# Linear attention in 64-wide TensorE tiles: one change to a fused patch, attention and expert kernel

## The chip, the cores and the metric

The kernel runs on one core of a Trainium2 chip. The metric is the time of one execution on the device, in microseconds (us); lower is better. Five engines work side by side and meet at semaphores: PE (TensorE: matmuls and transposes, with the load of their stationary operand listed apart as PEld), DVE (VectorE), ACT (ScalarE), POOL (GpSimd) and SP (which issues DMAs).

## The reference, cut to what matters

64 images of 96x96x3 are cut into 36 patches each and projected to 256 features; a class token and 77 text tokens are added, which makes 114 tokens an image. Then come a linear attention of 16 heads of 16 features, and 8 experts of which each token takes one. The part that the change touches is the middle of the attention:

```python
Q = _feature_map(Q)
K = _feature_map(K)
KV = jnp.einsum('bshd,bshe->bhde', K, V)
K_sum = K.sum(axis=1)
Z = 1.0 / (jnp.einsum('bshd,bhd->bsh', Q, K_sum) + 1e-06)
out = jnp.einsum('bshd,bhde,bsh->bshe', Q, KV, Z)
```

Each head needs only its own 16x16 block of keys times values.

## The kernel before

The images go in 32 pairs. Each engine runs `for i in range(PAIRS): step(i)`, a pipeline written out by hand: the PE `step` (L1482) holds, in this order, `rank(i - 4)`, `key_value(i - 1)`, `turn_attention(i - 2)`, `project(i)`, `project_out(i - 2)`, `apply(i - 1)`, `turn_tokens(i + 1)` and `queries(i)`. DVE (L1171) and ACT (L832) have lists of their own. Nothing is scheduled at run time: an engine waits at its next instruction until the semaphore arrives. After the pairs, 64 tiles of sorted tokens go through the experts (L1580, L1616).

- `key_value` (L1366) multiplies keys by values for an image b and a half c of the heads (8 heads, 128 features): the stationary operand is `k_sb` of 114 tokens x 128 features, and 136 columns of `v_sb` move: 128 values, and 8 ones that give the sums of the keys. Four such matmuls make a pair. They are f32, and each is two passes in the trace, with a load of its own for each pass.
- `masked` (L1030, DVE) multiplies the four 128 x 136 results by a mask that keeps the blocks of each head, into `kv_sb`.
- `apply` (L1429) multiplies queries (`qT`, 128 features x 114 tokens, stationary) by `kv_sb`, 136 columns moving, again four f32 matmuls of two passes.
- `denominators` (L805, ACT) and `attention` (L1078, DVE) take the last 8 columns of each result, invert them and scale the 128 others.
- Around them on PE: `rank` (L1359 to L1362, bf16), the transposes of `turn_attention` (L1389) and `turn_tokens` (L1451), and products of the fp32r kind, written as three matmuls (L1326 to L1328). `queries` writes its results to the bank `b_w`, which `residual` (L1054) and `gate_logits` (L1062) on DVE must have read; `key_value` and `rank` write to `b_att`, which `attention` must have read.
- In two steps there is small extra work on PE ahead of `rank`: `early_count` (L1472) and `early_slots` (L1479, L1480), whose results have 8 rows or 1.

Of the kernel before, what the change touches and what calls it, by code (L numbers as in the profile page):

```python
# [24 lines left out]
P = 128  # L25
# [11 lines left out]
HEADS = 16  # L37
DH = D // HEADS
HPC = P // DH
KVW = P + HPC  # L40
EXPERTS = 8
INNER = 128
REGION = TOKENS + P
# [16 lines left out]
Z_EPS = 1e-6  # L60

CONSTS = {
    "c_ident": (P, P), "c_earlier": (TOK, TOK), "c_mask": (P, KVW), "c_weight8": (TOK, EXPERTS),
    "c_region": (P, 2 * EXPERTS), "c_regcol": (EXPERTS, 1), "c_tri": (EXPERTS, ENDS_W), "c_gap": (EXPERTS, ENDS_W),
    "c_before": (EXPERTS, EXPERTS),
}
# [1 line left out]
SLOT_W = EARLY_TILES * EXPERTS + EARLY_TILES  # L68
ROW_SETS = [range(0, 1), range(1, 2), range(2, 3), range(3, 4), range(4, 6), *(range(n, min(n + 3, 32)) for n in range(6, 32, 3))]
KGW = D + EXPERTS  # L70
RANK_AT, EARLY_AT = KC * KVW, 320
DUO = 2
RESULT_RING = 8
DUOS = TILES // DUO
# [38 lines left out]
def build(nc, x, txt, w_tok, pos, wq, bq, wkgv, wo, wo_rows, bias, drop, bias_kv, bo_col, wgu_in, wdown_in, ids, consts, slots, out):  # L113
    scratch = nc.dram_tensor("sorted_rows", (EXPERTS * REGION + P, ROW), F32, kind="Internal").ap()

    with ExitStack() as ctx:
# [85 lines left out]
        with ExitStack() as room:  # L202
            q_exp = sb("q_exp", [P, KC, 2 * TOK], at=room)
            q_relu = sb("q_relu", [P, KC, 2 * TOK], at=room)
            qT = sb("qT", [P, KC, 2 * TOK], at=room)
            k_exp = sb("k_exp", [TOK, 2, D], at=room)
            k_sb = sb("k_sb", [TOK, 2, D], at=room)
            gate_part = sb("gate_part", [TOK, 4, 2, EXPERTS], at=room)
            v_sb = sb("v_sb", [TOK, 2, KC, KVW], at=room)
            kv_sb = sb("kv_sb", [P, 2, KC, KVW], at=room)  # L210
            den = sb("den", [TOK, 2, HEADS], at=room)
            z = sb("z", [TOK, 2, HEADS], at=room)
            attn = sb("attn", [TOK, 2, D], at=room)
            attnT_hi, attnT_lo = parts("attnT", [P, KC, 2 * TOK], room)
            rows = sb("rows", [TOK, 4, 2, ROW], at=room)
            stats2 = sb("stats2", [TOK, 2, 6], at=room)
            mv2 = sb("mv2", [TOK, 4, 2, 2], at=room)
            ve2 = sb("ve2", [TOK, 2], at=room)
            rstd2 = sb("rstd2", [TOK, 4, 2], at=room)
            mean_neg = sb("mean_neg", [TOK, 4, 2], at=room)  # L220
            ratio = sb("ratio", [TOK, 2], at=room)
            logits = sb("logits", [TOK, 2, 2, EXPERTS], at=room)
            top = sb("top", [TOK, 2, 2], at=room)
            top_n = sb("top_n", [TOK, 2, 2], at=room)
            ranked = sb("ranked", [TOK, 2, EXPERTS], at=room)
            first = sb("first", [TOK, 2], at=room)
            chosen = sb("chosen", [TOK, 2, 2, EXPERTS], BF16, room)
            tanh_top = sb("tanh_top", [TOK, 2, 2], at=room)
            route_w = sb("route_w", [TOK, 2], at=room)
            place_e = sb("place_e", [TOK, 2, EXPERTS], at=room)  # L230
            place_f = sb("place_f", [TOK, 4, 2], at=room)
            place = sb("place", [TOK, 4, 2], I32, room)

            xsT = sb("xsT", [P, 6, KC, P], at=room)
            silu_g = sb("silu_g", [P, 4, INNER], at=room)
            act_u = sb("act_u", [P, 4, INNER], at=room)
            actT = sb("actT", [P, 6, P], at=room)
            result = sb("result", [P, RESULT_RING, D], at=room)
# [15 lines left out]
        b_att = ps("b_att", [P, 2, 512])  # L254
        b_w = ps("b_w", [P, 2, 512])
        b_t = ps("b_t", [P, 512])

        b_x, b_gu = (b_v[:, :], b_t[:, :]), (b_kg[:, 0, :], b_kg[:, 1, :])

# [482 lines left out]
        def _(act):  # L742
# [54 lines left out]
            def values(p):  # L797

                act.wait_ge(kvp_done, p + 1)
                if p >= 1:  # L800
                    act.wait_ge(kvm_done, p)
                S.copy(v_sb[:, :, :, 0:P].rearrange("p b k e -> p (b k) e"),
                       b_v[0:TOK, :].rearrange("p (a e) -> p a e", e=P)).then_inc(v_ready, 1)

            def denominators(p):  # L805

                act.wait_ge(apply_done, p + 1)
                if p >= 1:
                    act.wait_ge(z_done, p)
                heads = b_att[0:TOK, :, 0:KC * KVW].rearrange("p b (k w) -> p b k w", k=KC)  # L810
                S.activation(den[:].rearrange("p b (k h) -> p b k h", k=KC), heads[:, :, :, P:KVW], ACT.Identity,
                             bias=z_eps[0:TOK, :]).then_inc(den_done, 1)

            def tokens_high(p):
# [122 lines left out]
        def _(dve):  # L937
# [92 lines left out]
            def masked(p):  # L1030

                dve.wait_ge(kvm_done, p + 1)
                if p >= 1:
                    dve.wait_ge(apply_done, p)
                V.tensor_tensor(kv_sb[:].rearrange("p b k w -> p (b k) w"),
                                b_att[:, :, 0:KC * KVW].rearrange("p b (k w) -> p b k w", k=KC),
                                mask.rearrange("p (a w) -> p a w", a=1).to_broadcast([P, 2 * KC, KVW]),
                                ALU.mult).then_inc(kv_ready, 1)

            def queries(p):  # L1040
# [37 lines left out]
            def attention(p):  # L1078
# [4 lines left out]
                dve.wait_ge(apply_done, p + 1)  # L1083
                if p >= 1:
                    dve.wait_ge(turn_attn_done, p)
                heads = b_att[0:TOK, :, 0:KC * KVW].rearrange("p b (k w) -> p b k w", k=KC)
                for b in range(2):
                    last = V.tensor_tensor(
                        attn[:, b, :].rearrange("p (k h e) -> p k h e", k=KC, h=HPC),
                        heads[:, b, :, 0:P].rearrange("p k (h e) -> p k h e", h=HPC),  # L1090
                        z[:, b, :].rearrange("p (k h a) -> p k h a", k=KC, a=1).to_broadcast([TOK, KC, HPC, DH]),
                        ALU.mult)
                last.then_inc(attn_ready, 1)

# [128 lines left out]
            def room_setup():  # L1223

                for n in (PT - 2, PT - 1):
                    patches_out(Turn(0, n))
                dve.wait_ge(patches_ready, PT)
                V.memset(v_sb[:, :, :, P:], 1.0)
                V.memset(rows[:, :, :, ID + 1:], 0.0).then_inc(room_ready, 1)

            units(dve, unit, [
# [88 lines left out]
        def _(pe):  # L1320
# [45 lines left out]
            def key_value(p):  # L1366
# [6 lines left out]
                    pe.wait_ge(attn_ready, p)  # L1373
                for b in range(2):
                    for c in range(KC):
                        last = T.matmul(b_att[:, b, c * KVW:(c + 1) * KVW], k_sb[:, b, c * P:(c + 1) * P],  # L1376
                                        v_sb[:, b, c, :], start=True, stop=True)
                last.then_inc(kvm_done, 1)

            def turn_attention(p):  # L1380
# [48 lines left out]
            def apply(p):  # L1429
# [4 lines left out]
                    pe.wait_ge(place_ready, p - 2)  # L1434
                for b in range(2):
                    for c in range(KC):
                        last = T.matmul(b_att[0:TOK, b, c * KVW:(c + 1) * KVW], qT[:, c, b * TOK:(b + 1) * TOK],  # L1437
                                        kv_sb[:, b, c, :], start=True, stop=True)
                last.then_inc(apply_done, 1)

            def turn_tokens(p):
# [236 lines left out]
def constants():  # L1678

    f = np.float32  # L1680
    d, h = np.arange(P), np.arange(HPC)
    own = (d[:, None] // DH == h[None, :]).astype(f)
    e = np.arange(EXPERTS)
    region = np.zeros((P, 2 * EXPERTS), f)
    region[TOK, 0:EXPERTS] = e * REGION
    tables = {
        "c_ident": np.eye(P, dtype=f),
        "c_earlier": np.triu(np.ones((TOK, TOK), f), 1),
        "c_mask": np.concatenate([np.repeat(own, DH, axis=1), own], axis=1),
        "c_weight8": np.tile((EXPERTS - e).astype(f), (TOK, 1)),  # L1690
        "c_region": region,
        "c_regcol": (e * REGION).astype(f)[:, None],
# [107 lines left out]
```

## Time and profile before

| | |
|---|---|
| median of 3 runs | 465.07 us (464.49 to 466.78) |
| the profiled execution's own time | 466.39 us |
| its span, first to last instruction | 464.6 us |
| PE busy | 442.6 us (95%) |
| DVE, POOL, ACT busy | 334.3, 291.5, 265.0 us |
| mean granted TensorE clock | 0.985 |

The profile follows one execution. Its span is the time from the first to the last instruction; the execution's own time has 1.8 us around that. Matmuls are pipelined: a matmul is listed from the moment that it is sent to the array to the moment that its last result is out, so neighbours overlap in the list. What a matmul costs the stream is the distance from its start to the start of the next, not its listed length.

### The profile page before, as it was taken

Reading aid. Unit: us, or ns where it says so; the run is one execution under the profiler, and the core shown is the slowest. Engines: PE = TensorE matmul, PEld = TensorE weight load, DVE = VectorE, ACT = ScalarE, POOL = GpSimd, SP = SyncE. Lnnn points to the kernel's source line nnn. Section 1 sums busy time; section 2 is a strip of 40 time slices with the busy share of each in tenths; the row PEclk is TensorE's granted clock in tenths of the full one; section 3 lists DMA queues with packets and bytes.
Section 4 is the critical chain, followed back from the end, with each engine's and each line's share of the span. In section 5 each row is a group of like instructions: output and inputs, shape, how many; then the busy total and the mean of one; then the engine's idle time right before and its main releaser. Section 6 shows DMA issues by size and latency. Waiting matters only on the chain.

```text
span 464.6 us, 11297 instructions
## 1 busy us (share of the span) xinstructions
PE 442.6 (95%) x3490; PEld 423.6 (91%) x3490; DVE 334.3 (72%) x1115; ACT 265.0 (57%) x640; POOL 291.5 (63%) x662
## 2 busy tenths in 40 slices
PE   8999999999999999999999999999879999999990
PEld 8999999999999999999999999999767888888870
DVE  6579468988888888888898888997665444434340
ACT  6354456766765766666676676556525444544430
POOL 5055223777777677677677777756557765656563
PEclk9999999999999999999999999999999999999995
DMA  8972221323222222122212111238314793221120
GB/s 295 333 222 98 58 56 50 102 80 100 78 78 72 59 61 64 39 81 82 70 36 52 54 36 38 65 104 224 107 43 129 242 293 112 79 71 65 65 80 18
DMA packets 34140, 46.34 MB, mean 100 GB/s; under 512 B 8842, under 2 KB 25856, under 8 KB 34082
## 3 DMA queue, kind: packets, MB, share of 16 engines
q1 hardware_dynamic: 24860, 30.50, 21.7%
q0 software_dynamic: 9216, 15.12, 10.3%
q8 instruction: 29, 0.48, 0.4%
q14 instruction: 29, 0.24, 0.2%
q10 hardware_dynamic: 6, 0.00, 0.0%
HBM read 26.87 MB, written 17.17 MB: 95 GB/s over the span
## 4 chain that ended last, share of the span: by engine, by line
PE 84%; DVE 4%; issue 3%; DMA 3%; ACT 2%; POOL 1%; SPq 0%; POOLq 0%; DVEq 0%
PE b_kg L1580 11%; PE b_att L1376 7%; PE b_w L1326 7%; PE b_w L1327 6%; PE b_w L1328 6%; PE b_att L1437 6%; PE b_kg L1326 4%; PE b_kg L1327 4%; PE b_kg L1328 4%; PE b_v L1328 3%; PE b_v L1327 3%; PE b_v L1326 3%; DMA rows_all<-in_x 3%; PE b_att L1616 3%; PE b_w L1616 3%
## 5 line engine op out<-in xcount | busy, mean ns | idle before, releaser
L655 POOL DMA_INDIRECT sorted_rows<-rows,place x64 | 75.5, 1180 | 20.5 <-POOL place L652 10.6
L733 POOL DMA_INDIRECT out<-result,rows_all x64 | 62.3, 973 | 36.6 <-DVE result L1256 24.4
L1580 PE MATMUL b_kg<-wgu,xsT 128*128 x256 | 66.1, 381 | 0.1
L1245 DVE SCALAR_TENSOR_TENSOR act_u<-b_kg,rows_all,silu_g 128x128 f32<-128x128 f32 x64 | 19.5, 346 | 57.1 <-ACT silu_g L912 57.1
L1580 PEld LDWEIGHTS b_kg<-wgu,xsT 128*128 128x128 f32 x256 | 43.8, 191 | 3.8 <-issue 0.2
L828 ACT ACTIVATE q_exp<-b_w,bq_s 128x228 f32<-128x228 f32 x64 | 28.9, 451 | 29.9 <-PE b_w L1328 29.9
L1326 PE MATMUL b_w<-wo_hi,attnT_hi 128*114 128x264 f32 x124 | 40.6, 328 | 0.0
L1326 PE MATMUL b_kg<-wkgv_hi,xnT_hi 128*114 128x264 f32 x128 | 38.8, 303 | 0.7 <-DVE patch_out L983 0.7
L1326 PE MATMUL b_w<-xnT_hi,wq_hi 128*128 128x256 f32 x128 | 38.5, 301 | 0.9 <-DVE logits L1067 0.6
L1437 PE MATMUL b_att<-kv_sb,qT 128*114 128x136 f32 x256 | 35.9, 285 | 1.9 <-DVE qT L1045 1.9
L1376 PE MATMUL b_att<-v_sb,k_sb 114*128 114x136 f32 x256 | 37.5, 289 | 0.0
L1327 PE MATMUL b_kg<-wkgv_lo,xnT_hi 128*114 128x264 f32 x128 | 36.4, 284 | 0.0
L1328 PE MATMUL b_kg<-wkgv_hi,xnT_lo 128*114 128x264 f32 x128 | 36.2, 283 | 0.0
L1328 PE MATMUL b_v<-wkgv_hi,xnT_lo 128*114 128x256 f32 x128 | 36.1, 282 | 0.0
L1326 PE MATMUL b_v<-wkgv_hi,xnT_hi 128*114 128x256 f32 x128 | 35.9, 281 | 0.0
L1327 PE MATMUL b_v<-wkgv_lo,xnT_hi 128*114 128x256 f32 x128 | 35.8, 280 | 0.0
L616 POOL TENSOR_SCALAR ve<-mv 114x2 f32<-114x2 f32 x32 | 7.3, 227 | 45.4 <-DVE mv L1000 45.4
L1327 PE MATMUL b_w<-xnT_lo,wq_hi 128*128 128x256 f32 x128 | 35.8, 279 | 0.0
L1327 PE MATMUL b_w<-wo_lo,attnT_hi 128*114 128x264 f32 x124 | 35.7, 288 | 0.0
L1328 PE MATMUL b_w<-xnT_hi,wq_lo 128*128 128x256 f32 x128 | 35.7, 279 | 0.0
L1328 PE MATMUL b_w<-wo_hi,attnT_lo 128*114 128x264 f32 x124 | 35.5, 286 | 0.0
L783 ACT ACTIVATE xn<-rows_all,shift,rstd 114x255 f32<-114x255 f32 x64 | 34.7, 591 | 0.2 <-POOL spread L604 0.2
(223 smaller groups left out, 1492.6 us busy)
## 6 DMA issues: line engine op xcount, KB each, us to landing
rows_all<-sorted_rows SPq DMA_DIRECT2D x64, 130.0 KB, 3.0
rows_all<-in_x SPq DMA_DIRECT2D x18, 384.0 KB, 5.1
rows_all<-in_txt SPq DMA_DIRECT2D x32, 154.0 KB
wgu<-in_wgu_in SPq DMA_DIRECT2D x8, 256.0 KB, 2.9
rows_all<-patch_out SPq DMA_DIRECT2D x48, 36.0 KB
sorted_rows<-tail_rows SPq DMA_DIRECT2D x9, 130.0 KB, 2.1
sorted_rows<-rows,place POOLq DMA_INDIRECT x64, 3.7
wdown<-in_wdown_in SPq DMA_DIRECT2D x2, 512.0 KB, 4.3
```

The costliest lines, as they stand in the source:

```text
L655: G.indirect_dma_start(out=scratch[0:EXPERTS * REGION, :], out_offset=bass.IndirectOffsetOnAxis(ap=place[:, k, b:b + 1], axis=0), in_=rows ...
L733: G.indirect_dma_start(out=out, out_offset=bass.IndirectOffsetOnAxis(ap=rows_all[:, t.n, ID:ID + 1].bitcast(I32), axis=0), in_=result[:, k ...
L783: last = S.activation(xn[:, b, 1:], rows_all[0:TOK, 2 * p + b, 1:D], ACT.Identity, bias=shift1[:, p % 8, b:b + 1], scale=rstd1[:, p % 8, b ...
L828: S.activation(q_exp[:, c, :], at, ACT.Exp, bias=bq_s[:, c:c + 1])
L1245: last = V.scalar_tensor_tensor(act_u[:, t.slot(4)], b_gu[m.slot(2)][:, up:up + INNER], rows_all[:, t.n, GAIN:GAIN + 1], silu_g[:, t.slot( ...
L1326: T.matmul(to, left_hi, right_hi, start=start, stop=False)
L1327: T.matmul(to, left_hi, right_lo, start=False, stop=False)
L1328: return T.matmul(to, left_lo, right_hi, start=False, stop=stop)
L1376: last = T.matmul(b_att[:, b, c * KVW:(c + 1) * KVW], k_sb[:, b, c * P:(c + 1) * P], v_sb[:, b, c, :], start=True, stop=True)
L1437: last = T.matmul(b_att[0:TOK, b, c * KVW:(c + 1) * KVW], qT[:, c, b * TOK:(b + 1) * TOK], kv_sb[:, b, c, :], start=True, stop=True)
L1580: last = T.matmul(to, xsT[:, t.slot(6), k, :], wgu[:, bass.ds(e, 1), k, :], start=(k == 0), stop=(k == KC - 1))
L1616: last = T.matmul(down_bank(m)[:, t.slot(2) * D:(t.slot(2) + 1) * D], actT[:, t.slot(6)], wdown[:, bass.ds(e, 1), :], start=True, stop=True)
```

## The change

Each 128-feature half is halved again. Keys times values becomes two matmuls of 114 x 64 (stationary) with 68 moving columns: 64 values and 4 ones. The first writes partitions 0 to 63 of the result, the second partitions 64 to 127, in the same columns of one bank. Queries times the result becomes two matmuls that contract over 64 rows each, partitions 0 to 63 and 64 to 127, with 68 columns moving, and they write to two different banks. The mask has 68 columns, and `masked` handles 4 x 68 columns in place of 4 x 136. So each stage has 8 matmuls of two passes, 16 passes with 16 loads, where it had 8 and 8.

```diff
+HALF = P // 2
+KVH = HALF + HPC // 2
...
-            v_sb = sb("v_sb", [TOK, 2, KC, KVW], at=room)
-            kv_sb = sb("kv_sb", [P, 2, KC, KVW], at=room)
-            den = sb("den", [TOK, 2, HEADS], at=room)
-            z = sb("z", [TOK, 2, HEADS], at=room)
+            v_sb = sb("v_sb", [TOK, 2, KC, 2, KVH], at=room)
+            kv_sb = sb("kv_sb", [P, 2 * KC, KVH], at=room)
+            den = sb("den", [TOK, 2 * KC, 2, HPC // 2], at=room)
+            z = sb("z", [TOK, 2 * KC, 2, HPC // 2], at=room)
...
+        b_kv = b_att[:, 0, 0:2 * KC * KVH].rearrange("p (a w) -> p a w", w=KVH)
...
-                S.copy(v_sb[:, :, :, 0:P].rearrange("p b k e -> p (b k) e"),
-                       b_v[0:TOK, :].rearrange("p (a e) -> p a e", e=P)).then_inc(v_ready, 1)
+                S.copy(v_sb[:, :, :, :, 0:HALF].rearrange("p b k j e -> p (b k j) e"),
+                       b_v[0:TOK, :].rearrange("p (a e) -> p a e", e=HALF)).then_inc(v_ready, 1)
...
-                V.tensor_tensor(kv_sb[:].rearrange("p b k w -> p (b k) w"),
-                                b_att[:, :, 0:KC * KVW].rearrange("p b (k w) -> p b k w", k=KC),
-                                mask.rearrange("p (a w) -> p a w", a=1).to_broadcast([P, 2 * KC, KVW]),
+                V.tensor_tensor(kv_sb[:], b_kv, mask.rearrange("p (a w) -> p a w", a=1).to_broadcast([P, 2 * KC, KVH]),
                                 ALU.mult).then_inc(kv_ready, 1)
...
-                for b in range(2):
+                by_half = attn[:].rearrange("p b (k j h e) -> p j (b k) h e", k=KC, j=2, e=DH)
+                for j in range(2):
                     last = V.tensor_tensor(
...
-                        last = T.matmul(b_att[:, b, c * KVW:(c + 1) * KVW], k_sb[:, b, c * P:(c + 1) * P],
-                                        v_sb[:, b, c, :], start=True, stop=True)
+                        for j in range(2):
+                            at = c * P + j * HALF
+                            last = T.matmul(b_kv[j * HALF:(j + 1) * HALF, b * KC + c], k_sb[:, b, at:at + HALF],
+                                            v_sb[:, b, c, j, :], start=True, stop=True)
...
-                        last = T.matmul(b_att[0:TOK, b, c * KVW:(c + 1) * KVW], qT[:, c, b * TOK:(b + 1) * TOK],
-                                        kv_sb[:, b, c, :], start=True, stop=True)
+                        a = b * KC + c
+                        for j in range(2):
+                            half = slice(j * HALF, (j + 1) * HALF)
+                            last = T.matmul(b_att[0:TOK, j, a * KVH:(a + 1) * KVH], qT[half, c, b * TOK:(b + 1) * TOK],
+                                            kv_sb[half, a], start=True, stop=True)
```

`denominators` reads the sums from the two banks in the new order. No wait and no semaphore is added, removed or moved.

## Rows read from the trace of the kernel before

**Rows 1.** The page: busy time, and the chain that ended last by engine.

```profile
PE 442.6 (95%) x3490; PEld 423.6 (91%) x3490; DVE 334.3 (72%) x1115; ACT 265.0 (57%) x640; POOL 291.5 (63%) x662
...
PE 84%; DVE 4%; issue 3%; DMA 3%; ACT 2%; POOL 1%; SPq 0%; POOLq 0%; DVEq 0%
```

**Rows 2.** Steady stretch: length, busy us of PE, PEld, DVE, ACT, POOL; clock; DMA.

```profile
94.00:200.00 106.00, 106.00 (x931) 105.86 (x931) 93.48 (x334) 70.67 (x180) 78.93 (x216) 1.00 0.24 69
```

**Rows 3.** Waits of PE over the whole span, longest first: us, times, longest.

```profile
PE b_att L1437 <- DVE qT L1045: 1.9, 1, 1.9
PE b_att L1359 <- DVE attnT_lo L942: 1.7, 1, 1.7
```

**Rows 4.** Timeline of PE matmuls, one step (columns: start us, us, what).

```profile
201.42 1.09 PE L1437 MATMUL b_att<-kv_sb,qT 128*114 128x136 f32 x8
202.35 0.56 PE L1451 MATMUL b_t<-con_s,xn 114*128 114x114 f32 x4
...
204.04 0.28 PE L1328 MATMUL b_w<-xnT_hi,wq_lo 128*128 128x256 f32 x1
...
204.36 1.17 PE L1376 MATMUL b_att<-v_sb,k_sb 114*128 114x136 f32 x8
205.37 0.56 PE L1389 MATMUL b_t<-con_s,attn 114*128 114x114 f32 x4
...
210.32 1.09 PE L1437 MATMUL b_att<-kv_sb,qT 128*114 128x136 f32 x8
```

**Rows 5.** The same step looked at alone: first matmul of L1376, and two loads.

```profile
204.36 0.36 PE L1376 MATMUL b_att<-v_sb,k_sb 114*128 114x136 f32 x1
...
204.13 0.13 PEld L1359 LDWEIGHTS b_att<-chosen,earlier 114*114 114x114 bf16 x1
...
202.64 0.19 PEld L1326 LDWEIGHTS b_w<-xnT_hi,wq_hi 128*128 128x128 f32 x1
```

**Rows 6.** Groups by line and form: loads of different widths (mean ns before the last bar).

```profile
L1376 PEld LDWEIGHTS b_att<-v_sb,k_sb 114*128 114x128 f32 x256 | 31.9, 190 | 0.0
L1451 PEld LDWEIGHTS b_t<-con_s,xn 114*128 114x128 f32 x128 | 14.5, 141 | 0.0
L1480 PEld LDWEIGHTS b_att<-early_f,con_s 8*8 8x8 f32 x2 | 0.1, 82 | 0.0
L1479 PEld LDWEIGHTS b_att<-con_s,early_f 8*1 8x1 f32 x2 | 0.1, 76 | 0.1
```

**Rows 7.** Timelines of the two steps with narrow matmuls ahead of `rank`.

```profile
284.42 0.09 PEld L1472 LDWEIGHTS b_att<-ones_bf,so_far 128*8 128x8 bf16 x2
...
284.21 0.28 PE L1328 MATMUL b_w<-xnT_hi,wq_lo 128*128 128x256 f32 x1
284.42 0.19 PE L1472 MATMUL b_att<-ones_bf,so_far 128*8 128x1 bf16 x2
...
284.77 0.36 PE L1376 MATMUL b_att<-v_sb,k_sb 114*128 114x136 f32 x1
...
293.35 0.28 PE L1328 MATMUL b_w<-xnT_hi,wq_lo 128*128 128x256 f32 x1
...
293.95 0.36 PE L1376 MATMUL b_att<-v_sb,k_sb 114*128 114x136 f32 x1
```

**Rows 8.** Timeline of DVE and ACT in the same step as rows 4.

```profile
201.62 0.69 DVE L1059 TENSOR_TENSOR rows<-b_w,rows_all 114x512 f32<-114x512 f32 x1 [0.40 <-PE b_w L1328]
202.23 0.35 DVE L1067 SCALAR_TENSOR_TENSOR logits<-b_w,rstd,gate_part 114x8 f32<-114x8 f32 x2
202.87 0.35 DVE L1081 RECIPROCAL z<-den 114x32 f32<-114x32 f32 x1 [0.29 <-ACT den L811]
203.25 0.76 DVE L1088 TENSOR_TENSOR attn<-b_att,z 114x256 f32<-114x256 f32 x2
...
202.55 0.29 ACT L811 ACTIVATE den<-b_att,z_eps 114x32 f32<-114x32 f32 x1 [1.23 <-PE b_att L1437]
```

**Rows 9.** Groups by line and form on DVE that read the attention's bank.

```profile
L1088 DVE TENSOR_TENSOR attn<-b_att,z 114x256 f32<-114x256 f32 x64 | 24.2, 420 | 1.1
L1035 DVE TENSOR_TENSOR kv_sb<-b_att,con_s 128x544 f32<-128x544 f32 x32 | 23.2, 724 | 6.0 <-PE b_att L1376 4.2
```

More of the change, by code:

```diff
@@ L62 @@
 CONSTS = {
-    "c_ident": (P, P), "c_earlier": (TOK, TOK), "c_mask": (P, KVW), "c_weight8": (TOK, EXPERTS),
+    "c_ident": (P, P), "c_earlier": (TOK, TOK), "c_mask": (P, KVH), "c_weight8": (TOK, EXPERTS),
     "c_region": (P, 2 * EXPERTS), "c_regcol": (EXPERTS, 1), "c_tri": (EXPERTS, ENDS_W), "c_gap": (EXPERTS, ENDS_W),
@@ L70 @@
 KGW = D + EXPERTS
-RANK_AT, EARLY_AT = KC * KVW, 320
+RANK_AT, EARLY_AT = 2 * KC * KVH, 320
 DUO = 2
@@ L809, in denominators @@
                     act.wait_ge(z_done, p)
-                heads = b_att[0:TOK, :, 0:KC * KVW].rearrange("p b (k w) -> p b k w", k=KC)
-                S.activation(den[:].rearrange("p b (k h) -> p b k h", k=KC), heads[:, :, :, P:KVW], ACT.Identity,
+                halves = b_att[0:TOK, :, 0:2 * KC * KVH].rearrange("p j (a w) -> p j a w", w=KVH)
+                S.activation(den[:].rearrange("p a j h -> p j a h"), halves[:, :, :, HALF:KVH], ACT.Identity,
                              bias=z_eps[0:TOK, :]).then_inc(den_done, 1)
@@ L1085, in attention @@
                     dve.wait_ge(turn_attn_done, p)
-                heads = b_att[0:TOK, :, 0:KC * KVW].rearrange("p b (k w) -> p b k w", k=KC)
-                for b in range(2):
+                by_half = attn[:].rearrange("p b (k j h e) -> p j (b k) h e", k=KC, j=2, e=DH)
+                for j in range(2):
                     last = V.tensor_tensor(
-                        attn[:, b, :].rearrange("p (k h e) -> p k h e", k=KC, h=HPC),
-                        heads[:, b, :, 0:P].rearrange("p k (h e) -> p k h e", h=HPC),
-                        z[:, b, :].rearrange("p (k h a) -> p k h a", k=KC, a=1).to_broadcast([TOK, KC, HPC, DH]),
+                        by_half[:, j],
+                        b_att[0:TOK, j, 0:2 * KC * KVH].rearrange("p (a w) -> p a w", w=KVH)[:, :, 0:HALF].rearrange("p a (h e) -> p a h e", e=DH),
+                        z[:, :, j, :].rearrange("p a (h o) -> p a h o", o=1).to_broadcast([TOK, 2 * KC, HPC // 2, DH]),
                         ALU.mult)
@@ L1227, in room_setup @@
                 dve.wait_ge(patches_ready, PT)
-                V.memset(v_sb[:, :, :, P:], 1.0)
+                V.memset(v_sb[:, :, :, :, HALF:], 1.0)
                 V.memset(rows[:, :, :, ID + 1:], 0.0).then_inc(room_ready, 1)
@@ L1682, in constants @@
     own = (d[:, None] // DH == h[None, :]).astype(f)
+    own_half = own[:, 0:HPC // 2] + own[:, HPC // 2:]
     e = np.arange(EXPERTS)
@@ L1688, in constants @@
         "c_earlier": np.triu(np.ones((TOK, TOK), f), 1),
-        "c_mask": np.concatenate([np.repeat(own, DH, axis=1), own], axis=1),
+        "c_mask": np.concatenate([np.repeat(own_half, DH, axis=1), own_half], axis=1),
         "c_weight8": np.tile((EXPERTS - e).astype(f), (TOK, 1)),
```

1 line of the change is left out of this document (removed).

## The prediction

> **What bounds the kernel now.** I read the page first. PE is busy for 95% of the span, and 84% of the chain that ended last is PE [rows 1]. [...] The list of waits agrees: PE waits for hardly anything, and its longest waits, 1.9 and 1.7 us, come once each [rows 3]; they lie in the last steps of the pairs. So in the steady part the time of a step is what PE needs to stream its list, 210.32 - 201.42 = 8.90 us a pair [rows 4]. Only what the change does to PE's stream counts at once; what it does to DVE counts where PE waits for DVE.
>
> Two stages of that stream change. `apply` reaches from 201.42 to the next transposes at 202.35: 0.93 us, 8 passes of 0.116. `key_value` reaches from 204.36 to 205.37: 1.01 us [rows 4]. That is 8 x 0.116 and 0.08 more, since the first pass is listed with 0.36 us where a pass takes 0.28: it waits there for its own load, which the short matmuls of `rank` can't cover [rows 4, 5]. In every other place a load lies under the matmul before it.
>
> **The unit prices.** A pass of 136 columns costs 0.116 us, so one of 68 columns is estimated at 0.058. A load of 1 column is listed with 76 ns and one of 128 with 190: 0.9 ns a column above a fixed part that is pipelined away [rows 6]. A load of 64 columns then holds its place for 0.058 us, one of 114 for 0.10; a load for a transpose, listed with 141, for 0.065 [rows 6].
>
> The trace has no 64-wide tile, but it has narrow ones. In two steps, matmuls with 1 or 8 result rows stand ahead of `rank`. From the last matmul of `queries` to the first of `key_value` a plain step takes 204.36 - 204.04 = 0.32 us [rows 4]; with two narrow matmuls (passes counted) it takes 284.77 - 284.21 = 0.56, with four 293.95 - 293.35 = 0.60 [rows 7]. The two more cost 0.04, so a narrow one 0.02, and 0.20 is left for going to another shape and coming back. One sees it happen: the load of L1472 starts 0.21 after the last full matmul started, in the plain step the next load after 0.09 [rows 4, 5, 7]. Of the 0.20, about 0.05 is the way back's uncovered load, listed with 0.13 against 0.08 for a narrow one [rows 5, 6]; that leaves 0.15 for the two drains themselves. Bounds for a round trip: 0, if a 64-wide shape drains nothing, and 0.20 with each side's uncovered loads on top. I take 0.15 with the loads that this change leaves uncovered, as the narrow matmuls are the nearest rows.
>
> [...]
>
> **Part by part.** How two 64-wide tiles share the array is shown nowhere, and is the open cost. From below: they overlap wholly, 8 pairs of passes. From above: nothing overlaps, 16 passes or 16 loads in a row. The two passes of one f32 matmul use one tile and must follow each other, so even with overlap only the second pass of one matmul runs beside the first of the next: 16 passes make 9 beats. I take this, near the lower end; the nearest row is that a load already runs beside a matmul today.
>
> - `key_value`: uncovered load 0.06, 9 beats x 0.058 = 0.52, drains 0.15, uncovered load of the transposes 0.065: 0.80 us against 1.01, a gain of 0.21. If nothing overlaps: 16 x 0.058 = 0.93 in place of 0.52, so 1.20, a loss of 0.19.
> - `apply`: its stationary operand still has 114 columns, so each of the 16 loads takes 0.10 while a pass has shrunk to 0.058; loads no longer lie under matmuls, they set the beat. With the loads of the two tiles side by side: first load 0.10, 8 beats x 0.10, last pass 0.06, drains 0.15, transposes' load 0.065: 1.18 us against 0.93, a loss of 0.25. With the loads in a row, 16 x 0.10 = 1.60 in place of 0.80: 1.98, a loss of 1.05.
> - `masked` on DVE: 128 x 544 takes 724 ns, 114 x 256 from the same bank 420, so 1.06 ns a column [rows 9]; 272 columns make 0.44 us, 0.29 less. In the steady part this is hidden behind PE. In the last steps, where PE waits for what stands behind `masked` in DVE's list (`attnT_lo`, `qT`) [rows 3], it comes through: two or three times 0.29, I take 0.6 us.
> - `attention`, `denominators`, the copy of the values and the ones: the same instructions, engines and element counts in another order, so nothing. Their cover: ACT idles 1.23 us before `den` [rows 8]. If strides cost DVE something, it is paid from the 0.29.
> - No wait and no DMA moves; the constants get 68 columns fewer. Nothing.
>
> Who comes next behind PE? `queries` on PE may start only when DVE has read `b_w`: the logits end at 202.23 + 0.35 = 202.58, and the first load of `queries` starts at 202.64 [rows 5, 8]. So `apply` can gain at most 0.06 us before PE waits there. A longer `apply` breaks nothing: `den`, `z` and `attn` (which ends at 203.25 + 0.76 = 204.01, ahead of 204.13 when `rank` loads) shift with PE [rows 5, 8].
>
> **Sum.** A pair: -0.21 + 0.25 = +0.04 us; 32 pairs +1.3; last steps -0.6: +0.7. The profiled execution took 466.39 us, so 467.1; the median of the runs is 1.3 below that execution, so 465.8. The two halves cancel.
>
> **The rivals.**
> - *The shape changes drain nothing.* Then `key_value` takes 0.06 + 0.52 = 0.58, a gain of 0.43, and `apply` gains its 0.06 at most, since the logits hold `queries`. 32 x 0.49 = 15.7, and 0.6: 448.8 us. For it: DVE has some 12% to spare [rows 2], so it can follow 0.49 us a pair. Against it: the 0.20 of the narrow matmuls.
> - *The loads go one after the other in both stages* (the slower side). The place is `apply`: 16 loads of 0.10 in a row. The price is 1.05 there and 0.19 in `key_value`: 32 x 1.24 = 39.7 less 0.6: 504 us. It decides as soon as `apply` takes more than 1.14 us, its 0.93 and the 0.21 that `key_value` gains. For it: all loads in the trace go in order, one at a time. Against it: all of those load the same array.
> - *The overlap is had in one stage only, or passes never overlap though loads do*: `key_value` at 1.20 (+0.19) and `apply` at 1.18 (+0.25) make 32 x 0.44 - 0.6 = +13.5, so 478.6 us; with the passes of `apply` in a row too (0.10 + 16 x 0.058 + 0.215 = 1.24) about 481. This includes the case that the tiles are only addressed and not run side by side. For it: two column tiles take the same rows of the array at the same moment. [...]
>
> **How the numbers follow.** About 0.5% (2.3 us) is what a measurement of this kernel can tell from no change. My forecast, cancellation, has a chance of 0.47; its own range is 459 to 471, as a beat or a drain mis-sized by 0.1 us in both stages makes 6 us; inside it I give faster 0.12, same 0.25, slower 0.10. No drain has 0.22, overlap in one stage only 0.20, loads in a row 0.11. So faster 0.12 + 0.22 = 0.34, same 0.25, slower 0.10 + 0.20 + 0.11 = 0.41. The range, 448 to 482, leaves out the loads in a row and the outer part of the first rival.
>
> **What would show it.** Right: `key_value` from its first matmul to the transposes near 0.8 us, `apply` near 1.2, loads of L1376 and L1437 in the new kernel overlapping each other in pairs, the load after each stage starting some 0.2 us after its last matmul, `masked` near 0.44. Wrong: an `apply` near 2 us (loads in a row); both stages near 0.6 with PE waiting for the logits (no drain); a step other than 8.9 us by more than 0.2.

## The result and the profile after

The changed kernel took 463.52 us (median of 7 runs, 462.02 to 465.52), the kernel before beside it 466.78 (7 runs, 464.49 to 468.25): 0.9929 of before, 95% interval 0.99 to 0.9958, a small gain of some 3.3 us. The forecast was 465.8 and "the two halves cancel". The profiled execution took 464.41 us with a span of 462.5; before, 466.39 and 464.6.

The page of the new kernel, busy time and chain by engine, answers to [rows 1]:

```profile
PE 441.4 (95%) x4002; PEld 412.6 (89%) x4002; DVE 321.5 (70%) x1115; ACT 262.4 (57%) x640; POOL 292.0 (63%) x662
...
PE 91%; DVE 2%; issue 2%; DMA 1%; POOL 1%; POOLq 0%; ACT 0%; SPq 0%; DVEq 0%
```

The same steady stretch, and then the stretch in which the pairs end and the experts begin (columns as in [rows 2]):

```profile
94.00:200.00 106.00, 106.00 (x1133) 102.03 (x1134) 89.43 (x338) 70.38 (x181) 80.90 (x217) 1.00 0.24 70
318.00:350.00 32.00, 26.15 (x214) 23.32 (x213) 19.95 (x91) 13.43 (x34) 17.05 (x50) 0.84 0.41 120
```

PE is as full as before, 106.00 of 106 us at the full clock, and still makes up the chain: a step is still what PE's list takes, and its two longest waits are 1.9 and 1.7 us as in [rows 3] (the first, ahead of the last `apply`, is put down to no engine now). The list has 512 more matmuls (two narrow ones for each wide one, 16 more a pair). The loads now leave PEld idle for 4 us in 106, where they left 0.14: those are the gaps at the changes of shape, 0.15 us ahead of each `apply` and 0.03 to 0.07 at each of the other edges of the two stages. DVE is 4.1 us less busy, nearly all of it the shorter mask.

The timeline of PE over one new step answers to [rows 4]:

```profile
202.58 0.28 PE L1328 MATMUL b_w<-xnT_hi,wq_lo 128*128 128x256 f32 x1
202.70 0.17 PE L1359 MATMUL b_att<-chosen,earlier 114*114 114x16 bf16 x1
...
202.96 0.69 PE L1378 MATMUL b_att<-v_sb,k_sb 114*64 114x68 f32 x16
203.58 0.61 PE L1391 MATMUL b_t<-con_s,attn 114*128 114x114 f32 x4
203.96 0.36 PE L1326 MATMUL b_kg<-wkgv_hi,xnT_hi 128*114 128x264 f32 x1
...
208.47 0.28 PE L1328 MATMUL b_w<-wo_hi,attnT_lo 128*114 128x264 f32 x1
208.69 1.02 PE L1442 MATMUL b_att<-kv_sb,qT 64*114 64x68 f32 x16
209.63 0.61 PE L1456 MATMUL b_t<-con_s,xn 114*128 114x114 f32 x4
210.01 0.37 PE L1326 MATMUL b_w<-xnT_hi,wq_hi 128*128 128x256 f32 x1
...
217.49 0.52 PE L1442 MATMUL b_att<-kv_sb,qT 64*114 64x68 f32 x6
```

The step is 217.49 - 208.69 = 8.80 us, where it was 8.90. Read start to start, and against the plain step of before:

| | before | after | difference |
|---|---|---|---|
| `rank` to `key_value` | 204.16 to 204.36: 0.20 | 202.70 to 202.96: 0.26 | +0.06 |
| `key_value` to its transposes | 1.01 | 0.62 | -0.39 |
| its transposes to the next projection | 0.32 | 0.38 | +0.06 |
| last projection to `apply` | 201.30 to 201.42: 0.12 | 208.47 to 208.69: 0.22 | +0.10 |
| `apply` to the transposes | 0.93 | 0.94 | +0.01 |
| transposes to `queries` | 0.32 | 0.38 | +0.06 |

`key_value` with its two edges gains 0.27, `apply` with its edges loses 0.17, and -0.10 is left: what is seen. From its first start to the transposes `apply` takes as long as before although it has twice the passes; the loss shows at its two edges.

The loads of the same step, each stage by itself:

```profile
202.96 0.55 PEld L1378 LDWEIGHTS b_att<-v_sb,k_sb 114*64 114x64 f32 x16
203.58 0.14 PEld L1391 LDWEIGHTS b_t<-con_s,attn 114*128 114x128 f32 x1
...
208.35 0.18 PEld L1328 LDWEIGHTS b_w<-wo_hi,attnT_lo 128*114 128x114 f32 x1
208.68 0.88 PEld L1442 LDWEIGHTS b_att<-kv_sb,qT 64*114 64x114 f32 x16 [0.15 <-issue]
```

A load of `key_value` is listed with 137 ns, one of `apply` with 177. Sixteen of them, one after the other at 0.059 and 0.100 (the pace that one tile keeps by itself in `same_tile` below), would reach over 15 x 0.059 + 0.137 = 1.02 and 15 x 0.100 + 0.177 = 1.68 us; eight pairs reach over 7 x 0.059 + 0.137 = 0.55 and 7 x 0.100 + 0.177 = 0.88. The rows say 0.55 and 0.88: two tiles load and multiply side by side from the first pass to the last, at 8 beats a stage. Taken one by one in the trace they say the same: in `key_value` the passes start at 203.069 and 203.076, then 203.128 and 203.135, two each 0.059 us.

So `key_value` has 8 beats of 0.059, 0.47 us where 8 passes of 0.116 took 0.93, and 0.19 of the difference goes at its edges: the gain of 0.27. `apply` has 8 beats of 0.100, 0.80 for 0.93, and its edges cost 0.30 more than before: the loss of 0.17.

The masked copy on DVE, by line and form, answers to the second row of [rows 9]:

```profile
L1037 DVE TENSOR_TENSOR kv_sb<-b_att,con_s 128x272 f32<-128x272 f32 x32 | 13.3, 415 | 2.0 <-PE b_att L1378 1.5 <-issue 0.2
```

**The end.** The last `key_value` starts at 327.00 where it started at 330.94, so 3.9 us are gained up to there; the span is shorter by 2.1 only. From that matmul to the first load of the experts it is 344.0 - 327.0 = 17.0 us, where it was 346.8 - 330.9 = 15.9; from there to the end 118.5 where it was 117.8. In between the granted clock is lower. In the kernel before the stretch from 318 to 350 had

```profile
318.00:350.00 32.00, 26.31 (x208) 24.61 (x207) 21.60 (x93) 14.04 (x36) 17.70 (x47) 0.95 0.41 116
```

a mean of 0.95 of the full clock, in the new one 0.84 (above): of four stretches of 4 us from 332 on, the old kernel had 0.84, 0.73, 1.00 and 1.00, the new one 0.61, 0.81, 0.76 and 0.67. PE is busy for about the same share of the 32 us in both, 26.31 and 26.15 us. The lower clock comes after the wait of 1.9 us ahead of the last `apply`, in both kernels: that wait ends at 334.8 and 330.9, and the stretch from 328 to 332 still has 1.00 and 0.96. The output product of the last pair, from its first to its last piece in the chain that ended last, in the kernel before:

```profile
342.33 0.16 PE b_att L1422
...
343.94 0.13 PE b_att L1328
```

In the new kernel:

```profile
338.39 0.15 PE b_att L1424
...
341.10 0.23 PE b_att L1328
```

It takes 1.74 and 2.94 us, since nearly all of its passes cost 0.22 in place of 0.12; the product before it takes 2.30 and 3.22 (from 336.96 and from 332.09), and the last `apply`, the other way round, 2.13 and 1.15. The sum, 1.2 + 0.9 - 1.0, is the 1.1 us given back before the experts: in these two profiles it is the clock.

### The profile page after: what moved, and what is told of

Read it like the earlier page. It is cut to its first block, busy times and chain, and to the rows that moved or that the text cites. A ratio compares the mean times of both kernels' runs of the same rounds, so it can differ in the third digit from the quotient of the medians.

```text
span 462.5 us, 12321 instructions
## 1 busy us (share of the span) xinstructions
PE 441.4 (95%) x4002; PEld 412.6 (89%) x4002; DVE 321.5 (70%) x1115; ACT 262.4 (57%) x640; POOL 292.0 (63%) x662
## 4 chain that ended last, share of the span: by engine, by line
PE 91%; DVE 2%; issue 2%; DMA 1%; POOL 1%; POOLq 0%; ACT 0%; SPq 0%; DVEq 0%
PE b_kg L1585 12%; PE b_w L1326 7%; PE b_w L1327 6%; PE b_w L1328 6%; PE b_att L1442 6%; PE b_kg L1326 5%; PE b_kg L1327 5%; PE b_kg L1328 4%; PE b_att L1378 4%; PE b_t L1456 4%; PE b_t L1391 4%; PE b_v L1328 3%; PE b_v L1326 3%; PE b_v L1327 3%; PE b_w L1621 3%; PE b_att L1621 3%
## 5 line engine op out<-in xcount | busy, mean ns | idle before, releaser
L1585 PE MATMUL b_kg<-wgu,xsT 128*128 x256 | 67.2, 386 | 0.1
L1326 PE MATMUL b_w<-wo_hi,attnT_hi 128*114 128x264 f32 x124 | 41.0, 331 | 0.0
L1326 PE MATMUL b_kg<-wkgv_hi,xnT_hi 128*114 128x264 f32 x128 | 39.0, 305 | 0.7 <-DVE patch_out L985 0.7
L1326 PE MATMUL b_w<-xnT_hi,wq_hi 128*128 128x256 f32 x128 | 38.6, 302 | 0.2
L1327 PE MATMUL b_kg<-wkgv_lo,xnT_hi 128*114 128x264 f32 x128 | 36.6, 286 | 0.0
L1326 PE MATMUL b_v<-wkgv_hi,xnT_hi 128*114 128x256 f32 x128 | 35.9, 280 | 0.0
L1327 PE MATMUL b_v<-wkgv_lo,xnT_hi 128*114 128x256 f32 x128 | 35.8, 280 | 0.0
L1327 PE MATMUL b_w<-xnT_lo,wq_hi 128*128 128x256 f32 x128 | 35.7, 279 | 0.0
L1327 PE MATMUL b_w<-wo_lo,attnT_hi 128*114 128x264 f32 x124 | 35.6, 287 | 0.0
L1442 PE MATMUL b_att<-kv_sb,qT 64*114 64x68 f32 x512 | 32.7, 267 | 1.9 <-issue 1.9
L1442 PEld LDWEIGHTS b_att<-kv_sb,qT 64*114 64x114 f32 x512 | 28.2, 176 | 6.9 <-issue 6.7
```

The source lines that it names most:

```text
L1326: T.matmul(to, left_hi, right_hi, start=start, stop=False)
L1327: T.matmul(to, left_hi, right_lo, start=False, stop=False)
L1442: last = T.matmul(b_att[0:TOK, j, a * KVH:(a + 1) * KVH], qT[half, c, b * TOK:(b + 1) * TOK], kv_sb[half, a], start=True, stop=True)
L1585: last = T.matmul(to, xsT[:, t.slot(6), k, :], wgu[:, bass.ds(e, 1), k, :], start=(k == 0), stop=(k == KC - 1))
```

## The experiments

The theory after the result: each tile runs its own 8 passes without waiting for the other, at a beat set by the longer of pass and load; each change of tile shape costs a delay of its own, the drain of the forecast; `key_value` gains more than that, `apply` gains less. Rivals: the gain comes from the shorter mask and not from PE; the two tiles overlap only by pairs of neighbouring passes (the 9 beats of the forecast); `apply` loses by something else than drains and loads; the time given back at the end is not the clock's.

### Each half alone

`kv_only` keeps `apply` at full width with the old mask of 544 columns; `apply_only` keeps `key_value` at full width, with the same old mask. Both keep the results of `key_value` in two banks, as in the kernel before.

```diff
 # kv_only: apply
-                        last = T.matmul(b_att[0:TOK, b, c * KVW:(c + 1) * KVW], qT[:, c, b * TOK:(b + 1) * TOK],
-                                        kv_sb[:, b, c, :], start=True, stop=True)
+                        last = T.matmul(b_att[0:TOK, b, 2 * c * KVH:2 * (c + 1) * KVH], qT[:, c, b * TOK:(b + 1) * TOK],
+                                        kv_sb[:, b, c].rearrange("p j w -> p (j w)"), start=True, stop=True)
 # apply_only: key_value
-                        last = T.matmul(b_att[:, b, c * KVW:(c + 1) * KVW], k_sb[:, b, c * P:(c + 1) * P],
-                                        v_sb[:, b, c, :], start=True, stop=True)
+                        last = T.matmul(b_att[:, b, 2 * c * KVH:2 * (c + 1) * KVH], k_sb[:, b, c * P:(c + 1) * P],
+                                        v_sb[:, b, c].rearrange("p j w -> p (j w)"), start=True, stop=True)
```

> Keys times values in two column tiles as in the changed kernel, queries times the result in full width as before, and the mask at its old length of 544 columns (the tiles write only the two diagonal quarters of each result; the mask makes zeros of the rest). Theory (PE's stream adds up: in the changed kernel the column tiles save about 0.26 us a pair with all their switches, the row tiles cost about 0.16): a step of 8.64 us where before has 8.91, so 31 x 0.26 = 8 us less, ratio 0.983. Rival 1 (the gain came from the shorter mask on DVE): the mask is not shorter here, so no gain, ratio 1.00, a step of 8.9. Rival 2 (DVE is the next bound): PE begins to wait in the steady steps, a step of 8.75 or more, ratio above 0.987.

> Keys times values in full width as before, queries times the result in two row tiles as in the changed kernel, the mask at its old length. Theory: the row tiles cost 0.16 us a pair, so 32 x 0.16 = 5 us more than before, ratio 1.011, a step of 9.06 us. Rival 1 (it is the mask that counts): ratio 1.00. Rival 3 (the row tiles save as the column tiles do, and the cost lies elsewhere): below 1.00.

`kv_only` took 460.14 us, 0.9826 of before (0.9775 to 0.9877); `apply_only` 471.09, 1.0084 (1.0053 to 1.0114). PE in a step of `kv_only`:

```profile
205.08 1.09 PE L1442 MATMUL b_att<-kv_sb,qT 128*114 128x136 f32 x8
206.01 0.56 PE L1456 MATMUL b_t<-con_s,xn 114*128 114x114 f32 x4
...
208.09 0.69 PE L1381 MATMUL b_att<-v_sb,k_sb 114*64 114x68 f32 x16
208.72 0.61 PE L1394 MATMUL b_t<-con_s,attn 114*128 114x114 f32 x4
...
213.74 1.09 PE L1442 MATMUL b_att<-kv_sb,qT 128*114 128x136 f32 x8
```

And in one of `apply_only`:

```profile
204.61 1.02 PE L1442 MATMUL b_att<-kv_sb,qT 64*114 64x68 f32 x16
205.56 0.61 PE L1456 MATMUL b_t<-con_s,xn 114*128 114x114 f32 x4
...
207.62 1.17 PE L1378 MATMUL b_att<-v_sb,k_sb 114*128 114x136 f32 x8
208.63 0.55 PE L1391 MATMUL b_t<-con_s,attn 114*128 114x114 f32 x4
...
213.69 1.02 PE L1442 MATMUL b_att<-kv_sb,qT 64*114 64x68 f32 x16
```

Steps of 8.66 and 9.08 us, -0.24 and +0.18 against 8.90. The stages have the lengths that they have together, 0.63 and 0.95. Both halves have the long mask, so their sum belongs beside `long_mask` below: -0.24 + 0.18 = -0.06 us a step, and that kernel's step of 8.83 is 0.07 under 8.90. The times agree less closely: -1.74% and +0.84% make -0.90%, and `long_mask` has -0.50% (-0.78 to -0.23); the intervals of the two halves, 0.5% and 0.3% to each side, cover the difference. So the change is a gain of about 8 us in one half and a loss of about 4 in the other; the better kernel is the half. The gain of `kv_only`, with the old mask, also rules out that PE's gain is the mask's.

### The mask

`long_mask` is the changed kernel with the mask of 544 columns again, and so with the results of `key_value` in two banks.

```diff
-                V.tensor_tensor(kv_sb[:], b_kv, mask.rearrange("p (a w) -> p a w", a=1).to_broadcast([P, 2 * KC, KVH]),
+                V.tensor_tensor(kv_sb[:].rearrange("p b k j w -> p (b k) (j w)"),
+                                b_att[:, :, 0:2 * KC * KVH].rearrange("p b (k w) -> p b k w", k=KC),
+                                mask.rearrange("p (a w) -> p a w", a=1).to_broadcast([P, 2 * KC, 2 * KVH]),
```

> The changed kernel with the mask at its old length of 544 columns, all else as in the changed kernel. Theory: the shorter mask counts only in the last steps of the pairs, where PE waits for DVE, so 0.6 us at most is lost: a step of 8.80 us, ratio to before 0.994. Rival 1 (the mask brings the gain): ratio 1.00, a step of 8.9.

It took 465.56 us, 0.995 (0.9922 to 0.9977), against 0.9929: the intervals overlap, so the traces decide. Groups on DVE by line and form, in this kernel:

```profile
L1037 DVE TENSOR_TENSOR kv_sb<-b_att,con_s 128x544 f32<-128x544 f32 x32 | 22.3, 698 | 1.8 <-PE b_att L1381 1.6
```

The mask is 0.28 us longer, and the steady step 8.83 in place of 8.80. These 0.03 are no wait of PE: they are spread over the passes of the projections, a few ns each, and whether the mask or the place of the data makes them is not shown. In the last steps, from one `apply` to the next `key_value`, the kernel before, `long_mask` and the changed one take 3.79, 3.78 and 3.48 us at one place (303.83 - 300.04, 301.80 - 298.02, 300.73 - 297.25) and 3.32, 3.15 and 3.08 a step later. So as a wait the mask comes through once in full and once by 0.07: 0.37 us; with the 0.03 of each step, some 0.8 in 31 steps, the long form costs 1.2 us.

### Is it the order of the tiles?

`same_tile` issues all passes of the first tile and then all of the second, in both stages.

```diff
-                for b in range(2):
-                    for c in range(KC):
-                        for j in range(2):
+                for j in range(2):
+                    for b in range(2):
+                        for c in range(KC):
```

> The changed kernel with the loop over the two halves outside, so that four matmuls of one tile follow each other, then four of the other. Theory (what runs side by side are neighbours in program order on different tiles): the pairs vanish but for the change of half; passes of keys times values start 0.058 us apart one by one (+0.47 us a pair of images), those of queries times the result 0.10 (+0.8 us): a step of about 10.0 us, some 35 to 40 us more than the changed kernel, about 500 us. Rival (the pairs are the two passes of one matmul, whatever its tile): no change, 463 us. Between them: loads overlap, passes don't.

One execution took 488.18 us, a step 212.04 - 202.49 = 9.55: slower, but not by as much as loads and passes in a row would make it (10.0 was expected). The loads of both stages in this kernel:

```profile
202.49 1.33 PEld L1442 LDWEIGHTS b_att<-kv_sb,qT 64*114 64x114 f32 x16 [0.15 <-issue]
...
206.03 0.84 PEld L1378 LDWEIGHTS b_att<-v_sb,k_sb 114*64 114x64 f32 x16
```

The loads of `key_value` that start up to 206.28, alone:

```profile
206.03 0.37 PEld L1378 LDWEIGHTS b_att<-v_sb,k_sb 114*64 114x64 f32 x5
```

Five loads in a row reach over 4 x 0.059 + 0.137 = 0.37: one tile's passes do come one per beat. But sixteen reach over 0.84 and 1.33 where a single file would take 1.02 and 1.68: the second tile's first load starts 0.29 us after the first tile's (0.46 in `apply`), while the first tile still works, and from there both run side by side. So the tiles are two streams of their own, and the second starts late, I infer, only because its instructions come later in the list. In the changed kernel they alternate, and nothing is held back: 8 beats, and not 9.

### The price of a drain, and what sets the beat of `apply`

To price the change of shape alone, `narrow8` puts one matmul of 1 column and 8 result rows ahead of `apply` in the kernel before; `narrow114` the same with 114 result rows, the shape of its neighbours. Nobody reads the result.

```diff
 # narrow8
+                T.matmul(b_att[0:8, 0, 400:401], ones_bf[:, 0:8], ones_bf[:, 0:1], start=True, stop=True)
 # narrow114
+                T.matmul(b_att[0:114, 0, 400:401], ones_bf[:, 0:114], ones_bf[:, 0:1], start=True, stop=True)
```

> The kernel before with one bf16 matmul of one column and 8 result rows ahead of queries times the result, in every pair, which nobody reads. Theory (going to another tile shape drains the array, some 0.095 us each way): from the last matmul of the output product to the first transpose it takes 0.19 us for the drains, 0.03 for the matmul and 0.10 for the load that nothing covers any more, 0.31 more in all: a step of 9.2 us, about 476 us. Rival (what the narrow matmuls of the trace cost was their waits): as the wide one, narrow114.

> The same with 114 result rows, so in the shape of its neighbours. Theory: no drain, only the matmul and the uncovered load: 0.12 us more, a step of 9.03 us, about 470.5 us. The difference to narrow8 is the price of two drains, 0.19 us a pair.

475.60 and 470.32 us (one execution each, the kernel before beside them 467.44), steps of 9.18 and 9.00, near what was expected. PE around the added matmul L1435 in `narrow8`:

```profile
205.51 0.28 PE L1328 MATMUL b_w<-wo_hi,attnT_lo 128*114 128x264 f32 x1
205.73 0.17 PE L1435 MATMUL b_att<-ones_bf 128*8 128x1 bf16 x1
205.83 1.18 PE L1438 MATMUL b_att<-kv_sb,qT 128*114 128x136 f32 x8
206.84 0.56 PE L1452 MATMUL b_t<-con_s,xn 114*128 114x114 f32 x4
```

The same place in `narrow114`:

```profile
201.58 0.28 PE L1328 MATMUL b_w<-wo_hi,attnT_lo 128*114 128x264 f32 x1
201.71 0.16 PE L1435 MATMUL b_att<-ones_bf 128*114 128x1 bf16 x1
201.73 1.16 PE L1438 MATMUL b_att<-kv_sb,qT 128*114 128x136 f32 x8
202.73 0.56 PE L1452 MATMUL b_t<-con_s,xn 114*128 114x114 f32 x4
```

From the last projection to the transposes: 206.84 - 205.51 = 1.33 and 202.73 - 201.58 = 1.15. The 0.18 between them is the round trip through another shape: 0.09 on the way in (0.22 against 0.13), 0.08 to 0.09 on the way back. It is the 0.10 at the way in that the table of the step shows for `apply`. All in all `narrow8`, with the loads that nothing covers and its narrow matmul, costs 9.18 - 8.90 = 0.28, next to the 0.30 at the edges of `apply`. "Drain" is the forecast's name for this delay; the rows show the 0.18 us, not what the array does meanwhile.

That leaves `apply` itself. `short_load` gives it 72 of the 114 tokens as the stationary operand, so its loads have 72 columns while the moved columns stay 68; the attention of the other 42 tokens is left out. `quads` does all the tokens in four tiles of 64 by 64, so that the loads have 64 and 50 columns.

```diff
 # short_load
-                            last = T.matmul(b_att[0:TOK, j, a * KVH:(a + 1) * KVH], qT[half, c, b * TOK:(b + 1) * TOK],
+                            last = T.matmul(b_att[0:72, j, a * KVH:(a + 1) * KVH], qT[half, c, b * TOK:b * TOK + 72],
                                             kv_sb[half, a], start=True, stop=True)
 # quads
-                            last = T.matmul(b_att[0:TOK, j, a * KVH:(a + 1) * KVH], qT[half, c, b * TOK:(b + 1) * TOK],
-                                            kv_sb[half, a], start=True, stop=True)
+                            for first, end in ((0, HALF), (HALF, TOK)):
+                                last = T.matmul(b_att[first:end, j, a * KVH:(a + 1) * KVH],
+                                                qT[half, c, b * TOK + first:b * TOK + end], kv_sb[half, a], start=True, stop=True)
```

> The changed kernel with only the first 72 of the 114 tokens in the stationary operand of queries times the result (it leaves out the attention of the other 42 tokens). Theory (the load sets the beat of the row tiles): the beat falls from 0.100 to 0.065 us, the stage by 8 x 0.035 = 0.28 us, a step of 8.52 us, some 8 us less than the changed kernel. Rival (the two row tiles share something else, or the matmuls set the beat): it stays at 0.100, a step of 8.80.

> The changed kernel with queries times the result in four tiles of 64 x 64: each of its matmuls split into tokens 0 to 63 and 64 to 113, which go to the two halves of the result's partitions. Theory (each tile is a stream of its own; in two row tiles a load of 114 columns, 0.10 us, sets the beat): with loads of 64 columns (0.058) the beat falls to 0.06, so the stage from its first matmul to the transposes falls from 0.95 us to 0.65: a step of about 8.55 us, some 8 us less than the changed kernel, PE waiting a little for the logits. [...]

`short_load` took 456.04 us and `quads` 458.15 (one execution each). The beat of 0.065 us expected of `short_load` is an estimate from [rows 6]: 72 columns at 0.9 ns. PE in a step of `short_load`:

```profile
205.04 0.74 PE L1443 MATMUL b_att<-kv_sb,qT 64*72 64x68 f32 x16
205.71 0.61 PE L1457 MATMUL b_t<-con_s,xn 114*128 114x114 f32 x4
...
213.64 0.74 PE L1443 MATMUL b_att<-kv_sb,qT 64*72 64x68 f32 x16
```

And in one of `quads`:

```profile
204.94 0.70 PE L1443 MATMUL b_att<-kv_sb,qT 64*64 64x68 f32 x32
205.57 0.61 PE L1457 MATMUL b_t<-con_s,xn 114*128 114x114 f32 x4
206.06 0.38 PE L1326 MATMUL b_w<-xnT_hi,wq_hi 128*128 128x256 f32 x1
...
213.56 0.70 PE L1443 MATMUL b_att<-kv_sb,qT 64*64 64x68 f32 x32
```

The loads of the stage in `short_load`:

```profile
205.04 0.60 PEld L1443 LDWEIGHTS b_att<-kv_sb,qT 64*72 64x72 f32 x16 [0.15 <-issue]
```

One of them is listed with 0.142 us, so eight pairs reach over 0.60 with (0.60 - 0.142) / 7 = 0.065 from pair to pair, where the changed kernel has (0.88 - 0.177) / 7 = 0.100. Taken one by one in the traces the beats are the same, 0.065 us with loads of 72 columns and 0.100 with 114. The rival, a beat that stays at 0.100 and a step of 8.80, falls: the moved columns are 68 in both kernels, and the beat follows the load, at 0.90 and 0.88 ns a column. `apply` takes 0.67 us in `short_load` and 0.63 in `quads`, from 0.94; the 0.27 gained in `short_load` are the 8 x 0.035 = 0.28 expected. In `quads` the beat is 0.059 with loads of 64 and of 50 columns alike: there a pass of 68 columns, estimated at 0.058 from the 0.116 of 136, is the longer one. Its 32 passes take no longer than the 16 of `key_value`, 0.63 us against 0.62, so four tiles run side by side. But the steps come out at 8.60 and 8.62, not at the 8.52 and 8.55 expected, and `short_load` and `quads` are 7.5 and 5.4 us below the changed kernel where some 8 were expected. The reason stands in `quads` between the transposes and `queries`: 206.06 - 205.57 = 0.49, where the changed kernel has 0.38. The logits on the timeline of DVE in `quads`:

```profile
205.66 0.35 DVE L1067 SCALAR_TENSOR_TENSOR logits<-b_w,rstd,gate_part 114x8 f32<-114x8 f32 x2
```

The first load of `queries` on the timeline of the loads:

```profile
206.06 0.19 PEld L1326 LDWEIGHTS b_w<-xnT_hi,wq_hi 128*128 128x128 f32 x1
```

The logits end at 206.01 and the load starts 0.05 later, as it did behind them before the change [rows 5, 8]; in the changed kernel the load starts 0.24 after them (209.99 against 209.75) and waits for nothing. So PE meets the limit that the forecast had named, `queries` behind the logits, and some 0.1 us of the gain in `apply` is lost there.

### The clock at the end

Each fill puts 102 matmuls that nobody reads at the three places where PE waits in the last steps, so that it does not stand idle there; in the kernel before, in the changed one, in `kv_only`, and last in `quads`.

```diff
+            def fill(count):
+
+                for _ in range(count):
+                    T.matmul(b_kg[0:TOK, 0, 300:300 + TOK], ones_bf[:], ones_bf[:], start=True, stop=True)
...
+            fill(30)
             apply(PAIRS - 1)
...
+            fill(40)
             rank(PAIRS - 2)
...
+            fill(32)
             rank(PAIRS - 1)
```

> The kernel before with the same extra matmuls at the same places. Theory: before loses less to the clock (0.73 to 0.84 between 332 and 340 us, 1.00 after that), so 1 to 2 us go: 465 us; and the changed kernel with them is then faster than this one by the whole 3.5 to 4 us that its pairs save. Rival: no change, 466.7, and the distance of the two stays 3.2 us.

> The changed kernel with 102 bf16 matmuls that nobody reads, put ahead of three waits of PE between the last pairs and the experts (30, 40 and 32 of them), so that PE doesn't idle there. Theory (the clock gives a part of the gain back: the last keys times values of the changed kernel start 3.9 us earlier than before, but its span is only 2.1 us shorter, and between 332 and 348 us the granted clock is 0.61 to 0.81): the clock stays at 1.00 there and 2 to 4 us go, 460 to 461.5 us, ratio to before 0.987. Rival (the handover is bound by waits for DVE and loads, the clock costs nothing): 463.5 us, or more if the extra matmuls are in the way.

> Column tiles for keys times values alone, as in kv_only, with the same extra matmuls. Theory: the gain of kv_only over before, 8.1 us, and 2 to 4 us of the clock: 456 to 458 us, ratio 0.979. Rival: as kv_only, 460.

> The kernel with apply in four tiles of 64x64, and the 102 unread matmuls of bf16 at the three places where PE waits in the last steps. If the handover from the pairs to the experts costs this kernel the same granted clock as the others, the matmuls give back 2 to 4 us of the 458.15 us of the run without them: 454 to 456 us, 0.976 of the kernel before, a mean granted clock near 0.988, and this is the fastest of all. Rival: with apply this short PE has idle time ahead of queries in every step anyway, and the handover is no longer what it loses: then 458 us, 0.982, and no faster than keys times values in column tiles with the same filling matmuls (457.5).

Each beside the kernel before in the same runs: `before_fill` 464.55 us, 0.9963 (0.9943 to 0.9983); `after_fill` 460.69, 0.9889 (0.9847 to 0.9931); `kv_fill` 457.52, 0.9815 (0.9773 to 0.9857); `quads_fill` 455.34 (454.75 to 456.28, 6 runs), 0.9751 (0.9716 to 0.9785). The stretch from 318 to 350 in `before_fill`:

```profile
318.00:350.00 32.00, 31.25 (x319) 29.67 (x318) 22.79 (x97) 15.07 (x39) 18.51 (x49) 1.00 0.46 132
```

In `after_fill`:

```profile
318.00:350.00 32.00, 29.94 (x326) 27.40 (x323) 21.78 (x98) 15.65 (x43) 20.42 (x56) 1.00 0.40 118
```

In `quads_fill`:

```profile
318.00:350.00 32.00, 29.62 (x336) 26.49 (x333) 20.95 (x90) 14.18 (x38) 20.40 (x50) 1.00 0.31 95
```

The clock is 1.00 in all three; without the fill the same stretch has 0.95 in the kernel before, 0.84 in the changed one and 0.84 in `quads`. So with PE kept busy over its waits the clock does not fall there. Each kernel comes out lower with the fill. For the kernel before, the interval (0.9943 to 0.9983) lies below 1; for the others (0.9889 against 0.9929, 0.9815 against 0.9826, and 455.34 us against a single 458.15) the intervals overlap or there is but one execution. With the clock equal, the two kernels stand 464.55 - 460.69 = 3.9 us apart, and without the fill 3.3: the direction fits, but the difference of 0.6 lies within the intervals. The clocks of the executions point the same way: the seven of the changed kernel have means of 0.978 to 0.985, the median 0.980, and the 38 of the kernel before that stood beside the experiments 0.978 to 0.989, the median 0.985. That the change itself costs clock at the end is thus seen in its profile and likely from the clocks, but not shown by the times. `quads_fill` is the fastest of all and beats both kernels; its gain over `kv_fill`, 0.9751 against 0.9815, is as expected, though the two intervals touch, and the rival for it, no gain from the clock, would have given 458.

## Why the prediction was wrong

The forecast was that the halves cancel, +0.04 us a pair; measured is -0.10. The mechanisms were the ones that the runs show; the terms of the sum were mis-sized, in both stages to the same side.

- **The bound** was right: PE is full before and after, so the change in PE's list is the change of the step.
- **`key_value`: "16 passes make 9 beats", because "the two passes of one f32 matmul use one tile and must follow each other, so even with overlap only the second pass of one matmul runs beside the first of the next".** This step failed. The two passes of a matmul do follow each other, 0.059 us apart, but the tiles don't wait for each other: the first passes of both start at 202.96, and each runs its 8 passes, two streams as `same_tile` shows. 8 beats of 0.059 are 0.47 in place of 0.52; the gain with edges is 0.27 in place of 0.21.
- **`apply`: 1.18 us, a loss of 0.25.** This term failed too, in its size. Load-bound, with loads side by side at 0.100 a beat: right, as `short_load` (0.065 with 72 columns) and `quads` (0.059 with 64) show. But the sum had "first load 0.10, 8 beats x 0.10, last pass 0.06", and the 8 loads are the 8 beats: the first was counted twice. Without it 1.08; measured is 0.93 + 0.17 = 1.10.
- **The drains:** 0.15 a round trip was a little low; `narrow8` against `narrow114` has 0.18. With the beats put right, 0.15 gives the 0.74 that `key_value` takes with its edges, and 0.18 the 1.10 of `apply`. The rival without drains falls by the same number, and the rivals with loads or passes in a row by the 8 beats in both stages.
- **The mask:** 0.44 us forecast, 0.415 on the mean of all and 0.41 in a plain step. In the last steps I took 0.6 for it; it came through once and a bit, 0.37, and the long form costs 0.03 in a plain step, where I took nothing. The last five steps (from the sixth last `key_value` to the last, 46.18 us before and 44.58 after) in all gained 1.6, which is 1.1 more than five plain ones; beyond the mask's 0.37 no run takes this apart.
- **The limit behind PE**, the logits, was rightly named: it costs nothing here and shows as soon as `apply` gets shorter.
- **What the sum lacked** is the end: the last `key_value` is 3.9 us earlier, but 1.1 us go again before the experts' first load and 0.7 after it. I took the stretch behind the pairs as fixed; in this profile it has a lower clock.

With the ninth beat and the doubled load put right and nothing else changed, the forecast's own sum is -0.27 + 0.15 = -0.12 a pair, 32 x -0.12 - 0.6 = -4.4 us: inside its own range of the cancelling case, and on the right side of it. What was at fault was to call two terms of 0.2 that almost cancel a sum of nothing: the error of each, 0.06 and 0.08, was larger than what was left. That the time came out only 2.3 us from the forecast is in part luck: the 1.8 us lost at the end, for which the sum had no term, hide a part of what the pairs gained beyond it.

## What to carry to other kernels

Price a change of tile shape by its round trip, here 0.18 us and the loads that it leaves uncovered, and split an operand only where the stage gains more than that. Between the edges the beat of a tile was in these runs the longer of its pass and its load: 0.116 us for a pass of 136 columns; with passes of 68 columns 0.100 and 0.065 over loads of 114 and 72, and 0.059 over loads of 64. Here, where only the blocks on the diagonal are wanted, both splits halve the moved columns; splitting the rows leaves the load of 114 columns, and the beat falls only from 0.116 to 0.100 us, less than its edges cost, while splitting the columns halves the load too, 0.116 to 0.059. Four tiles of 64 by 64 shorten both, to a beat of 0.059 in `quads`. Where two parts of one change are of opposite sign and nearly equal, build each alone before the whole.

## What the runs showed of the hardware that was not expected

Two column tiles load at the same time though they take the same rows: 16 loads of 137 ns within 0.55 us. They also overlap matmuls of the same 114 rows: the loads reach from 202.96 to 203.51, the passes from 202.96 to 203.65. The forecast had the shared rows as a point for a rival, while the kernel before already runs a load beside a matmul of the same rows at full width: at 201.06 a load of L1327 with 128 rows starts together with the matmul of L1326 ahead of it, of 128 rows too.

The tiles are in order each by itself, not among each other: in `same_tile` the second tile's loads start 0.29 us after the first tile's, ahead of the last two loads of the first tile, which stand before them in the list.
